# Graph products of the first layer done in step two of the top-p attention only

## What is computed

```python
R = S + eye(N);  R = R / R.sum(-1)            # S is the adjacency
Xf = Xa = X
for n in range(2):                            # two steps
    A = top_p_attention(Xa, W1, W2, W3)       # N x N, row softmax, rows cut to 90% of their mass
    Xf = R @ Xf                               # one hop of the graph product
    Xa = A @ Xa
    Z = Z + Xf @ U1[n].T + Xa @ U2[n].T
h = layernorm(X + Z)
```

## Time and profile before

| what | us |
|---|---|
| median of 3 runs | 3660.4 |
| lowest and highest | 3637.91, 3662.38 |
| the profiled execution | 3661.14 |
| its span | 3658.4 |
| busy PE, DVE, ACT, POOL over the span | 2394.6, 2690.6, 1057.6, 121.1 |
| pairs of step one | about 80.6 to 679 |
| projections and first logits of step two | 680.6 to 732 |
| pairs of step two | 732 to 2303 |
| layer normalization, then the second layer | 2304 to 3658 |

### The profile page before, as it was taken

The page is one execution under the profiler, slowest core; times in us unless marked ns, Lnnn a source line. Parts: engine busy times, 40 slices in busy tenths (PEclk is TensorE's granted clock), DMA queues, the critical chain, the costliest instruction groups (busy, mean ns, idle before and its releaser), DMA issues. The chain is left out here.

```text
span 3658.4 us, 58243 instructions
## 1 busy us (share of the span) xinstructions
PE 2394.6 (65%) x18628; PEld 2066.9 (56%) x18628; DVE 2690.6 (74%) x8845; ACT 1057.6 (29%) x1636; POOL 121.1 (3%) x295
## 2 busy tenths in 40 slices
PE   5899999734555511345323155399889999999774
PEld 2677777423444411234212144399879999999663
DVE  3656665298898986988886899654389999999335
ACT  3555555421222210212111121100044344443221
POOL 0000000000000000000000000000000000000000
PEclk9999999967777755677666677588799999999887
DMA  3122222111111100111010110244323333333100
GB/s 111 63 76 76 76 76 76 38 38 38 38 38 38 38 1 0 38 38 38 1 38 1 38 39 1 97 168 168 127 97 118 114 133 132 115 116 114 65 0 19
DMA packets 53628, 241.14 MB, mean 66 GB/s; under 512 B 5799, under 2 KB 17068, under 8 KB 39532
## 3 DMA queue, kind: packets, MB, share of 16 engines
q1 hardware_dynamic: 53356, 238.53, 18.6%
HBM read 233.40 MB, written 5.11 MB: 65 GB/s over the span
## 5 line engine op out<-in xcount | busy, mean ns | idle before, releaser
L716 PE MATMUL tr<-ident,e 128*128 128x128 f32 x1352 | 223.4, 297 | 843.2 <-DVE scalars L946 841.9
L716 PEld LDWEIGHTS tr<-ident,e 128*128 128x128 f32 x1352 | 175.3, 154 | 854.5 <-DVE scalars L946 850.7
L1430 PE MATMUL a_acc<-H,pT 128*128 128x128 f32 x4056 | 547.8, 277 | 11.6 <-ACT a_rows L1462 3.6
L1430 PEld LDWEIGHTS a_acc<-H,pT 128*128 128x128 f32 x4056 | 495.3, 192 | 28.6 <-DVE pT L1564 16.2
L67 DVE MAX8 cand<-e 128x8 f32<-128x32 f32 (+1 forms) x3042 | 366.5, 201 | 184.9 <-issue 184.8
L842 ACT ACTIVATE wT<-tr 128x512 f32<-128x512 f32 (+1 forms) x364 | 202.6, 566 | 809.4 <-PE tr L716 808.7
L730 PE MATMUL accA<-XR,wT 128*128 128x128 f32 x2704 | 380.4, 288 | 8.2 <-ACT wT L842 8.2
L730 PEld LDWEIGHTS accA<-XR,wT 128*128 128x128 f32 x2704 | 347.8, 202 | 20.6 <-ACT wT L842 20.6
L677 PE MATMUL lg<-kT,qs 128*128 128x512 f32 (+1 forms) x728 | 323.2, 596 | 47.8 <-ACT e L807 38.1
L1564 DVE TENSOR_TENSOR pT<-a_tr,a_adjT 128x512 f32<-128x512 f32 (+1 forms) x546 | 316.3, 644 | 20.3 <-PE a_tr L1389 16.8
L688 PE MATMUL accR<-XR,adj 128*128 128x129 f32 x2704 | 315.1, 276 | 22.1 <-ACT rawR L829 21.6
(11 more groups left out here) (311 smaller groups left out, 2879.3 us busy)
## 6 DMA issues: line engine op xcount, KB each, us to landing
adj<-in_adjT SPq DMA_DIRECT2D x52, 1664.0 KB, 6.8
g_adj<-in_adjT SPq DMA_DIRECT2D x26, 1664.0 KB, 6.9
a_adj<-in_adj SPq DMA_DIRECT2D x26, 1664.0 KB, 6.8
a_adjT<-in_adjT SPq DMA_DIRECT2D x156, 256.0 KB, 3.9
a_adjT<-in_adjT SPq DMA_DIRECT2D x26, 128.0 KB, 4.1
XT<-in_x_t SPq DMA_DIRECT2D x1, 1664.0 KB, 13.3
nsT_scratch<-nsT SPq DMA_DIRECT2D x1, 1664.0 KB, 5.3
gsT_scratch<-a_gs SPq DMA_DIRECT2D x26, 64.0 KB, 1.6
```

The costliest lines, as they stand in the source:

```text
L716: mm = eng.transpose(tr[(k * NC + c) % 2][:, o:o + P], e[b][k][:, j * P:(j + 1) * P], ident[:, :])
L1430: mm = eng.matmul(acc[:, :], pT[g % RING][:, (j % 4) * P:(j % 4 + 1) * P], H[:, j, :], start=(j == 0), stop=(j == T - 1))
```

## The change

Step one does no hop any more. In step two, every pair does the rows of two units (a unit is a row pair of one hop, `u` from 0 to 25): unit 0 comes before the first pair, the pairs 0 to 5 do units 1 to 12 (first hop), pair 6 does unit 13, and the pairs 7 to 12 do units 14 to 25 (second hop, scaled with the inverses kept from the first). The row itself is added by a matmul with the identity as the first of its group, no longer by POOL. The share of U1 has its own products, copies and additions to H. In the order of the engines, these move: in step one, PE turns the flags of the next pair between its attends as before, while DVE now goes search, tops of the next pair's block 0, read flags, both selects, tops of block 1, sort; DVE, before the first search of step two, inverts the row sums of unit 0. In step two the pairs are now in two loops with written-out pairs between and after them. The first two repeat rounds of a row block are in a loop of their own. The diff, cut to its core:

```diff
@@ -437,7 +437,9 @@
             eng.reg_mov(flag, kind)
             with eng.If(eng.snap(kind) > OPEN - 1):
                 eng.drain()
-                another()
+                with eng.Fori(0, 2):
+                    with eng.If(eng.snap(flag) > OPEN - 1):
+                        another()
                 while_over(eng, flag, OPEN - 1, self.width // 8, another)
                 eng.drain()
                 self.find_ties(eng, k)
...
+        def units_of(p, hop):
+
+            if hop == 0:
+                return [(p * 2 + 1, 1), (p * 2 + 2, 0)]
+            if hop == 1:
+                return [(p * 2, 0), (p * 2 + 1, 1)]
+            return [(PAIRS, 1)]
+
+        def over_pairs_with_rows(eng, pair):
+
+            with eng.Fori(0, TURN // 2) as pp:
+                pair(pp * 2, 0, 3, 0)
+                pair(pp * 2 + 1, 1, 3, 0)
+            pair(TURN, TURN % 2, 3, 2)
+            with eng.Fori(0, (PAIRS - TURN - 3) // 2) as pp:
+                pair(pp * 2 + TURN + 1, (TURN + 1) % 2, 3, 1)
+                pair(pp * 2 + TURN + 2, TURN % 2, 3, 1)
+            for p in range(TURN + 1 + (PAIRS - TURN - 3) // 2 * 2, PAIRS):
+                pair(p, p % 2, PAIRS - 1 - p, 1)
+
+        def hop_of(hop):
+            return 0 if hop == 0 else 1
...
+                for hop in range(2):
+                    with eng.Fori(0, PAIRS) as q:
                         for k in range(2):
 
-                            eng.wait_ge(adj_free, seq(step, p, k) + 1)
-                            eng.dma_start(adj[k][:, :], d["adjT"][bass.ds((p * 2 + k) * P, P), :]).then_inc(adj_loaded[k], 16)
-
-                eng.wait_ge(added, 2 * PAIRS + 1)
+                            eng.wait_ge(adj_free, seq(hop, q, k) + 1)
+                            eng.dma_start(adj[k][:, :], d["adjT"][bass.ds((q * 2 + k) * P, P), :]).then_inc(adj_loaded[k], 16)
+
+                eng.wait_ge(addedA, 2 * PAIRS)
+                eng.wait_ge(addedR, UNITS)
...
+                    def scale_rows(u, s):
+
+                        eng.wait_ge(inv_ready, u + 1)
+                        for k in range(2):
+                            eng.tensor_tensor(rawR[s][k][:, 0:P], rawR[s][k][:, 0:P],
+                                              inv_sums[:, bass.ds(u * 2 + k, 1)].to_broadcast([P, P]), ALU.mult)
+                        eng.drain()
+                        eng.sem_inc(rowR_ready, 2)
+                        for k in range(2):
+                            eng.tensor_copy(XR[2][:, bass.ds(u * 2 + k, 1), 0:P], rawR[s][k][:, 0:P].unsqueeze(1))
+                        eng.drain()
+                        eng.sem_inc(hop_done, 1)
+
+                    def add_rows(u, hop):
+
+                        q = u - hop * PAIRS
+                        eng.wait_ge(zsR_ready, u + 1)
+                        eng.tensor_tensor(H[:, bass.ds(q * 2, 2), :], H[:, bass.ds(q * 2, 2), :], zsR[:, :, :], ALU.add)
+                        eng.drain()
+                        eng.sem_inc(addedR, 1)
 
...
+                    def pair_with_rows(p, b, rest, hop):
+                        if rest >= 2:
+                            give_q(p + 2, 0)
+                            give_q(p + 2, 1)
+                        if hop == 0:
+                            for u, s in units_of(p, hop):
+                                scale_rows(u, s)
+                        for u, s in units_of(p, hop):
+                            add_rows(u, hop_of(hop))
                         give_attended(p)
 
                     for p in range(2):
...
+                    def rows(u, hop):
+
+                        xf = XR[0] if hop == 0 else XR[2]
+                        for k in range(2):
+                            eng.wait_ge(adj_loaded[k], (u + 1) * 16)
+                            eng.wait_ge(accR_read, u * 2 + k + 1)
+                            eng.matmul(accR[:, :], ident[:, :],
+                                       xf[:, bass.ds((u - hop * PAIRS) * 2 + k, 1), :].rearrange("p a n -> p (a n)"),
+                                       start=True, stop=False)
+                            for j in range(T):
+                                mm = eng.matmul(accR[:, :], adj[k][:, j * P:(j + 1) * P], xf[:, j, :],
+                                                start=False, stop=(j == T - 1))
+                            mm.then_inc(accR_ready, 1)
+                            eng.drain()
+                            eng.sem_inc(adj_free, 1)
+
+                    def turn_rows(u, s):
+                        eng.wait_ge(rowR_ready, u * 2 + 2)
+                        for k in range(2):
+                            mm = eng.transpose(xt[:, k, :], rawR[s][k][:, 0:P], ident[:, :])
+                        mm.then_inc(xtR_ready, 1)
+
+                    def update_rows(u, hop):
+                        eng.wait_ge(xTR_ready, u + 1)
+                        for k in range(2):
+                            mm = eng.matmul(zp[:, k, :], xT[:, k, :], UT[:, 0, hop, :], start=True, stop=True)
+                        mm.then_inc(zR_ready, 1)
 
...
                     def pair(p, b, rest):
-                        rows(p, 0)
-                        rows(p, 1)
-                        if step == 1:
-                            turn_flags(p)
                         attend(p, b, 0)
-                        if step == 0 and rest:
+                        if rest:
                             turn_flags(p + 1)
-                        turn_rows(p)
                         attend(p, b, 1)
                         if rest >= 2:
                             logits(p + 2, 0)
...
+                    def pair_with_rows(p, b, rest, hop):
+                        units = units_of(p, hop)
+                        if hop == 2:
+                            eng.wait_ge(hop_done, PAIRS + 2)
+                        for u, s in units:
+                            rows(u, hop_of(hop))
+                        turn_flags(p)
+                        attend(p, b, 0)
+                        eng.wait_ge(zsA_ready, turn_of(step, p) + 1)
+                        turn_rows(*units[0])
+                        attend(p, b, 1)
+                        if rest >= 2:
+                            logits(p + 2, 0)
+                            logits(p + 2, 1)
+                        update_rows(units[0][0], hop_of(hop))
+                        for u, s in units[1:]:
+                            eng.wait_ge(zsR_ready, u)
+                            turn_rows(u, s)
+                            update_rows(u, hop_of(hop))
+                        eng.wait_ge(zsR_ready, units[-1][0] + 1)
+                        turn_attended(p)
+                        update(p)
+
+                    eng.wait_ge(addedA, step * PAIRS)
                     for c in range(NC):
                         project(0, W1T[:, :], XT[:, cols(c)], c)
                     for c in range(NC):
...
+                    else:
+                        rows(0, 0)
+                        eng.wait_ge(zsA_ready, PAIRS + 1)
+                        turn_rows(0, 0)
+                        update_rows(0, 0)
+                        eng.wait_ge(zsR_ready, 1)
+                        over_pairs_with_rows(eng, pair_with_rows)
 
...
+                    def copy_rows(u, s, hop):
+
+                        if hop == 0:
+                            eng.wait_ge(hop_done, u + 1)
+                        for k in range(2):
+                            eng.wait_ge(accR_ready, u * 2 + k + 1)
+                            if hop == 0:
+                                eng.activation(rawR[s][k][:, :], accR[:, :], ACT.Copy).then_inc(accR_read, 1)
+                            else:
+                                eng.activation(rawR[s][k][:, 0:P], accR[:, 0:P], ACT.Copy,
+                                               scale=inv_sums[:, bass.ds((u - PAIRS) * 2 + k, 1)])\
+                                   .then_inc(accR_read, 1)
+                        if hop:
+                            eng.drain()
+                            eng.sem_inc(rowR_ready, 2)
+
...
+                    def copy_update_rows(u):
+                        eng.wait_ge(zR_ready, u + 1)
+                        eng.wait_ge(addedR, u)
+                        eng.activation(zsR[:, :, :], zp, ACT.Copy).then_inc(zsR_ready, 1)
 
...
+                    def pair_with_rows(p, b, rest, hop):
+                        units = units_of(p, hop)
+                        for u, s in units:
+                            copy_rows(u, s, hop_of(hop))
+                        if rest:
+                            exps(p + 1, 1 - b, 0)
+                            exps(p + 1, 1 - b, 1)
+                            exp_tops(p + 1)
+                        copy_attended(p, b, 0)
+                        copy_turned_rows(units[0][0])
+                        copy_attended(p, b, 1)
+                        if rest >= 2:
+                            copy_logits(p + 2, b, 0)
+                            copy_logits(p + 2, b, 1)
```

(92 more changed lines are left out.)

114 lines of the change are left out of this document (42 added, 72 removed).

## The result

The changed kernel took 3700.1 us (median of 4 runs, 3687.3 to 3701.4) against 3653.5 for the kernel before in the same comparison (4 runs, 3637.9 to 3662.4): a ratio of 1.0124, 95% interval 1.0079 to 1.017. Slower is clear; by how much over 1% is not. The forecast was 3712 us, range 3670 to 3748. The profiled execution took 3699.3 us with a span of 3697.7.

What follows compares the result with a forecast made beforehand. Step one was taken as bound by PE, with a loop of waits deciding once work left, and step two by DVE. Terms 26.0 + 27.8 + 1 + 2.2 - 6.0 + 0 = +51 on 3661.1 gave 3712 us, range 3670 to 3748.

Steps and rivals of the forecast that it cites:

- Step one: Head, ten middle pairs and tail of step one, summed as a serial loop of waits across engines: +26.0 us.
- edge: DVE's loop edge: 2.1 us in every second pair of step one; three instead of five in step two, -6.0.
- restart: PE's slower row block after idling about 11 us in each pair of step one: 1.9 us per pair.
- Start of step two: DVE's first search of step two waits for PE's rows of unit 0 and their inverses: +27.8 us.
- Step two's pairs: Extra PE work fits the slack before DVE reads the flags, except +1 us in the last pair; edges -6.0.
- the repeat rounds: Repeat rounds of step two's row blocks: 13.2 us saved, +3 and +10 lost, together 0.
- The empty second pass: In four row blocks with one round, the new loop's extra pass costs 2.5 us each, +10 together.
- Rival 1: Same chain in step one without restarts and edges: 3679 us, +0.5%; chance 0.23.
- Rival 2: Step one bound by PE at 33.5 us a pair, flags ready when attend 0 ends: 3511 us, faster; chance 0.08.
- Rival 3: Row blocks of step two run at 1.2 GHz, 12 us each, making PE late: 3910 us; chance 0.04.

Runs made afterwards that it cites:

- pads: Changed kernel with two extra DVE passes in every pair of step one: before the search 3740.1 us, behind the search 3687.1 us (one run each).
- kept busy: Changed kernel with 84 unused identity transposes on PE between attend 0 and the turn of the flags in step one: 3681.1 us, ratio 1.0062.
- moved: Changed kernel with PE turning the next pair's flags behind attend 1 in step one, DVE's new order kept: 3628.0 us, ratio 0.9929.
- one move: Changed kernel with the rows of unit 0 done between the logits of pair 0 and pair 1 in step two: 3671.1 us, ratio 1.0049.
- DVE ahead: Changed kernel with DVE's earlier order in step one (both selects before the next pair's tops), flags still turned between the attends: 3669.5 us, ratio 1.0041.
- DVE ahead and flags moved: Changed kernel with DVE's earlier order in step one and PE turning the flags behind attend 1: 3624.8 us, ratio 0.9934.

## Why the prediction was right, and where a size was off

**Step one, right.** It was read as a loop of waits rather than from busy shares: +25.3 measured against +26.0. The runs show its members one by one: DVE before the search (pads), PE's attend 1 (kept busy), the place of the flags (moved). Inside, small sizes erred against each other. A pair without an edge took 50.6 us, not 50.2: from the tops of block 1 to the search DVE needs 12.2 us, where the sum has 11.7. Over an edge this stretch takes 14.2 us, so the edge itself costs the 2.0 that was priced at 2.1. But such a pair takes 51.8, only 1.2 more, since its attend 1 restarts faster (11.1 us instead of 11.7) and its tops of block 1 come 0.4 us sooner behind those of block 0. In the kept-busy run, where attend 1 mostly takes 9.7 us with and without the edge, the two kinds of pair differ by 1.7. Why PE restarts faster in the pair over the edge, after a longer wait (12.7 us instead of 11.1), no run shows. That the mean period came out as forecast (51.2 against 51.25) is so in part luck.

**Start of step two, right,** 27.6 against 27.8, and undone by one move.

**Step two's pairs, right on the rows, wrong on the rounds.** The extra 17 us of PE fitted into the slack as read, with the 1 us in the last pair. The edges gave what was priced: five of 2.8 to 3.1 us before, three of 2.9 to 3.0 after, -5.9. The term that was mis-sized is the repeat rounds, put at 0. Exits of a block with one round and with two, changed kernel, DVE:

```profile
1836.33 0.24 DVE L382 TENSOR_SCALAR hits<-index,scalars 128x24 f32<-128x24 f32 x1 [3.52 <-issue]
...
2009.67 0.24 DVE L382 TENSOR_SCALAR hits<-index,scalars 128x24 f32<-128x24 f32 x1 [5.40 <-issue]
```

The empty second pass that I priced at 2.5 us costs nothing. The four blocks with one round leave with 4.8, 5.9, 3.5 and 3.5 us of idleness instead of 4.9, 4.7, 4.9 and 4.8. Counted from the L382 ahead of the rounds to the one behind them, these four take 163.3 us together instead of 163.5, the block with two rounds 75.5 instead of 88.3, and the one with three 123.4 instead of 121.0. That is 10.6 us gained instead of 0, and undoing the edit gave 11.8 back. With the edges it makes -16.5, and the twelve pairs gained 12.8: the rest, +3.7, is spread over the pairs (those without rounds and with the same edges grew by 0.3 to 0.7 us, 90.2 to 90.9 the most) and was not isolated. So of the 12 us between forecast and trace 7 lie in these pairs and 4 in the second layer, whose code is the same.

The Trainium skill's rule on taken branches (Runtime: NRT & Kernel Launch, "Instruction fetch mechanics"), read so that every jump of the empty pass has to wait for a fetch, would have had these four blocks cost 24 us more; the trace goes against that reading. The page says it only of targets outside the two pages in hand, and no run shows where these targets lie.

**Rivals.** Rival 1 (no restart, no edge) is refuted by the clock of 0.83, by the kept-busy run and by the 2.0 us of the edge. Rival 2, PE-bound step one at 33.5 us, needed the flags 11 us sooner; even with the flags out of the way the period was 44, and 40 with a full clock, since ACT's exponentials stand between PE's transposes and matmuls. The Trainium skill (Perfetto Trace Analysis, "Optimization Strategy") says that interleaving regimes may improve performance; here it did so only after the order around it had been changed too (3700.1 us without, 3628.0 with the flags moved, 3658.4 before). Rival 3 did not occur: most row blocks of step two ran in 6.0 us, as in flow, the first of a pair in up to 8.7, none in 12.

## What to carry to other kernels

Work taken off the busiest engine shortens a stage only as far as the next loop of waits allows: add up one turn of it (who waits for whom until the same point of the next turn) before trusting busy shares. After removing work from between two waits, look whether the wait on the other side now stands in the way, and move it behind work that doesn't need it; here one line moved was worth about 70 us. The first unit of moved work needs a place of its own, in an idle stretch ahead of the engine that bounds the next stage.

## What was not expected

- With the flags behind attend 1, PE waits 3.1 to 3.5 us for ACT twice in a pair, and its next matmuls ran at about half speed for some 5 us each time (mean clock 0.89); with the waits filled the clock was 1.00 and the pair 4.4 us shorter. But such a wait alone does not do it. With DVE ahead and the flags between the attends, PE waits just as long ahead of attend 0 and goes on at full speed in every inner pair; there attend 1 was the slow one, behind 9.2 us:

```profile
388.64 1.16 PE L785 MATMUL accA<-XR,wT 128*128 128x128 f32 x8 [3.29 <-ACT wT L937]
```

What makes the difference between these two runs was not isolated.
- The second layer is the same code in all kernels, and took 1326 to 1354 us in the profiled executions. In its graph sums, 70 us at the same distance behind the end of the first layer, the kernel before and the run with DVE ahead and flags moved:

```profile
2434.00:2504.00 70.00, 65.77 (x925) 65.26 (x922) 32.39 (x42) 2.92 (x21) 0.00 (x0) 0.85 0.48 170
```

```profile
2408.00:2478.00 70.00, 65.44 (x1056) 64.86 (x1055) 38.59 (x50) 3.34 (x24) 0.00 (x0) 1.00 0.57 204
```

PE was as busy in both, at a clock of 0.85 in the one and 1.00 in the other, and did 1056 matmul instructions instead of 925. No edit touches this code, and the difference of up to 28 us is as large as the whole range of the kernel before (3638 to 3662), so I take it to go with the execution; two traces of one kernel, which would show it, were not compared, and what decides it was not tried. It is also why gains of step one and two are better read up to the end of the first layer than from the total.
- POOL was busy 78.9 us in the inner pairs of step one after the change, against 45.2 before with more instructions. With DVE's new order and the flags moved it was 86.3, and with DVE ahead 21.6, for 64 and 60 instructions (both from 110 to 600 us). Its additions to H took 4.1 us where they ran beside the selects of DVE, and 0.73 with DVE ahead; why was not isolated. The same flags moved with either order of DVE gave the same period, so this cost nothing in time.
